# The order of the last root, the last stores and the last scalings at the end of a routed decoder kernel

## Chip, cores and metric

The kernel runs on one core of a Trainium2 chip. The metric is the device time of one execution in microseconds (us), as the median of several executions. Times "in the span" are counted from the first instruction of the profiled execution. PE is TensorE, DVE is VectorE, ACT is ScalarE, POOL is GpSimd, SP is SyncE.

## What is computed

1024 tokens of width 256 go through attention with a residual and a layer norm, a per-token choice of one of four experts by token id with residual and layer norm, and a feed-forward layer in which a router chooses one of four experts. The part that matters here is the last layer norm:

```python
def _layernorm(x, axis=-1, eps=1e-05):
    m = jnp.mean(x, axis=axis, keepdims=True)
    v = jnp.var(x, axis=axis, keepdims=True)
    return (x - m) / jnp.sqrt(v + eps)

x = _layernorm(x + _L0_ffn_ref(x, Wr, br, Wg, Wu, Wd), axis=-1)
```

## The kernel before

The tokens of the last layer lie sorted by expert in T = 10 tiles of 128 rows. Each tile passes four quarters of the feed-forward width; the fourth quarter ends a tile, and only there is the last layer norm done, tile by tile, in the order `last_order` = 0 to 5, 9, 6, 7, 8. The text numbers the tiles by their place n in this order, from 0 to 9, so "row block 7" is the eighth to finish. (The title of the change counts from one: its seventh tile is n = 6, its eighth n = 7, its ninth n = 8.)

For each n the work is spread over three engines, and every engine runs its own list strictly in the order in which it was written out by hand:

- DVE adds PE's product to the sum (`finish_sum`, L1520), takes the row statistics (`finish_stats`, L1526), makes mean and variance of them and adds epsilon (`finish_variance`, L1529 and L1247, which signals `var_ready`, or `last_var` for n = 8 and 9).
- For n = 0 to 7, POOL raises the variance to the power -0.5 (`root`, L500, into `rstd`, signals `rstd_ready`); DVE forms the shift, minus mean times that root (`finish_norm`, L1545, signals `nmr_ready`); ACT scales and shifts the rows (`norm_row`, L1114, signals `out_ready`).
- For n = 8 and 9 (the last `ROOTS_BY_ACT` = 2) ACT takes the square root instead (L1143, into `sroot`, signals `last_root`), for which it has switched its table with a small dummy Sqrt at L1138. DVE takes the reciprocal (L1537) and scales the rows itself (L1538; both `finish_row`, which signals `last_ready`).
- POOL sends every block to its tokens' places in memory with an indirect store (L577), which waits for `out_ready` or `last_ready`.

`mv`, `rstd` and `nmr` have two buffers, used in turn by n. POOL's list in the kernel before takes root n + 1 ahead of store n, for n = 0 to 6; at its end it reads: root 6, store 5, root 7, store 6, store 7, store 8, store 9. ACT's list at its end reads: scaling 6, dummy Sqrt with its table load, scaling 7, root 8, root 9. DVE's list reads: sum 8, statistics 8, shift 7, variance 8, sum 9, statistics 9, scaling 8, variance 9, scaling 9. SP waits for all ten stores (L438), and this ends the kernel.

Of the kernel before, what the change touches and what calls it, by code (L numbers as in the profile page):

```python
# [31 lines left out]
T = MOST - 1  # L32
# [35 lines left out]
def route_kernel(nc, aw, xT_in, x_in, ids_in, wr_in, br_in, ctx_in, ctxn_in, wffn_in, out):  # L68
# [3 lines left out]
    with ExitStack() as ctx:  # L72
# [190 lines left out]
        ROOTS_BY_ACT = 2  # L263


        LN1, LN3 = 0, CHUNKS
# [57 lines left out]
        def pieces_beside(j):  # L324
            q, n = divmod(j, T)
            if q == NQ - 1:
                return range(0)
            a = (q + 1) * Q_PIECES + sum(share[q][:n])
            return range(a, a + share[q][n])
# [112 lines left out]
        def _(pool):  # L442
# [55 lines left out]
            def root(n, buf, i):  # L498
                pool.wait_ge(var_ready, n + 1)
                g.tensor_tensor(out=rstd[:, buf, i:i + 1], in0=mv[:, buf, i, 1:2], in1=mhalf[:, 0:1],  # L500
                                op=ALU.pow).then_inc(rstd_ready, 1)
# [66 lines left out]
                    split(k)  # L568
            root(LN3, 0, 0)
            for n, t in enumerate(last_order):  # L570
                if n + 1 < T - ROOTS_BY_ACT:
                    root(LN3 + n + 1, (n + 1) % 2, 0)
                if n < T - ROOTS_BY_ACT:
                    pool.wait_ge(out_ready, n + 1)
                else:
                    pool.wait_ge(last_ready, n + 1 - (T - ROOTS_BY_ACT))
                g.indirect_dma_start(out=out, out_offset=bass.IndirectOffsetOnAxis(ap=outidx[:, t:t + 1], axis=0),  # L577
                                     in_=buf[:, t, 0:D], in_offset=None, bounds_check=TOKENS - 1,
                                     oob_is_err=False).then_inc(d_out, 16)


        @block.tensor
# [364 lines left out]
        def _(act):  # L947
# [27 lines left out]
            def split(k):  # L975

                n, _, src, hi, _ = all_pieces[k]
                if n == BESIDE:
                    act.wait_ge(d_beside, 16 * PIECES)
                else:  # L980
                    act.wait_ge(d_chunk[slot(n)], 16 * filling(n))
                if n >= E:
                    act.wait_ge(y_done, T + (n // E - 1) * T - 1)
                a(hi, src, ACT.Copy).then_inc(split_hi, 1)  # L984
# [105 lines left out]
            def fxhi(t):  # L1090
                act.wait_ge(x_done, T + t + 1)
                if t == JOINT:
                    a(x_joint[:, 0:P], fX[t % 2][:, 0:P], ACT.Copy).then_inc(xhi_done, 1)
                else:
                    a(x2s(t, 0), fX[t % 2][:, 0:D], ACT.Copy).then_inc(xhi_done, 1)

            def fsilu(j):
                act.wait_ge(g_done, T + j + 1)
                act.wait_ge(h_done, T + j - 1)
                a(gate[:, (T + j) % 2, :], fA[j % 2][:, 0:FQ], ACT.Silu).then_inc(silu_done, 1)  # L1100

            def fhhi(j):
                act.wait_ge(ht_done, T + j + 1)
                act.wait_ge(y_done, T + j - 1)
                if items[j][1] == JOINT:
                    a(h_joint[:, 0:P], fH[j % 2][:, 0:P], ACT.Copy).then_inc(hhi_done, 1)
                else:
                    a(hT[:, j % 2, 0, :], fH[j % 2][:, 0:FQ], ACT.Copy).then_inc(hhi_done, 1)  # L1108

            def norm_row(n):  # L1110

                t = last_order[n]
                act.wait_ge(nmr_ready, n + 1)
                a(buf[:, t, 0:D], buf[:, t, 0:D], ACT.Identity, bias=nmr[:, n % 2:n % 2 + 1],  # L1114
                  scale=rstd[:, n % 2, 0:1]).then_inc(out_ready, 1)

            fxhi(0)
            for i in range(len(items) + 4):
                if i == EARLY:
                    fhhi(i - 1)  # L1120
                    fxhi(i)
                    fxhi(i + 1)
                    fsilu(i)
                else:
                    if i + 1 < JOINT and i + 1 != EARLY:
                        fxhi(i + 1)
                    if i < len(items):
                        fsilu(i)
                    if i + 1 == JOINT:
                        fxhi(i + 1)  # L1130
                    if 1 <= i <= len(items):
                        fhhi(i - 1)
                n = i - 3 - (len(items) - T)
                if 0 <= n < T - 4:
                    norm_row(n)
                if n == T - 3:
                    norm_row(n - 1)
                    a(lsum[:, 0:1], ones_f[:, 0:1], ACT.Sqrt)  # L1138
                if n == T - 2:
                    norm_row(n - 1)  # L1140
                    for k in range(ROOTS_BY_ACT):
                        act.wait_ge(last_var, k + 1)
                        a(sroot[:, k:k + 1], mv[:, (T - ROOTS_BY_ACT + k) % 2, 0, 1:2], ACT.Sqrt).then_inc(last_root, 1)  # L1143
                if i < len(items):
                    for k in pieces_beside(i):
                        split(k)
# [3 lines left out]
        def _(dve):  # L1150
# [3 lines left out]
            def step(ins):  # L1154

                steps[0] += 1
                ins.then_inc(dve_step, 1)
                dve.wait_ge(dve_step, steps[0])
# [87 lines left out]
            def variance_eps(buf, i):  # L1246
                return v.scalar_tensor_tensor(out=mv[:, buf, i, 1:2], in0=mv[:, buf, i, 1:2], scalar=EPS,  # L1247
                                              in1=ones_f[:, 0:1], op0=ALU.add, op1=ALU.mult)
# [150 lines left out]
            def late_blocks(a, b):  # L1399
                block_table(a, b, a - EARLY, nth_by_size[:], 2 * BLOCKS)  # L1400
# [79 lines left out]
            def fhlo(j):  # L1480
                dve.wait_ge(hhi_done, j + 1)
                if items[j][1] == JOINT:
                    v.tensor_copy(h_joint[:, P:FQ], fH[j % 2][:, P:FQ]).then_inc(hlo_done, 1)
                    return
                v.tensor_tensor(out=hT[:, j % 2, 1, :], in0=fH[j % 2][:, 0:FQ],  # L1485
                                in1=hT[:, j % 2, 0, :].bitcast(F32), op=ALU.subtract).then_inc(hlo_done, 1)
# [41 lines left out]
            def finish_variance(n):  # L1528
                step(v.bn_aggr(mv[:, n % 2, 0, :], stats[:, n % 2, :]))  # L1529
                variance_eps(n % 2, 0).then_inc(last_var if n >= T - ROOTS_BY_ACT else var_ready, 1)  # L1530
# [10 lines left out]
            def finish_norm(t):  # L1541
                dve.wait_ge(rstd_ready, LN3 + t + 1)
                if t >= 2:
                    dve.wait_ge(out_ready, t - 1)
                v.scalar_tensor_tensor(out=nmr[:, t % 2:t % 2 + 1], in0=mv[:, t % 2, 0, 0:1], scalar=-1.0,  # L1545
                                       in1=rstd[:, t % 2, 0:1], op0=ALU.mult, op1=ALU.mult).then_inc(nmr_ready, 1)

            for i in range(len(items) + 3):
                if i == EARLY:
                    fhlo(i - 1)  # L1550
                    fxlo(i)
                    fxlo(i + 1)
                    fhidden(i)
                else:
                    if 1 <= i and i + 1 < JOINT and i + 1 != EARLY:
                        fxlo(i + 1)
                    if i == 1:
                        late_blocks(LATE, MOST)
                    if i < len(items):
                        fhidden(i)  # L1560
                    if i + 1 == JOINT:
                        fxlo(i + 1)
                    if 1 <= i < len(items):
                        fhlo(i - 1)
                if i == 1:
                    late_rows(LATE, MOST)
                if 2 <= i <= len(items) + 1 - T:
                    fsum(i - 2)
                if i == T - 1:
                    shifted_logits()  # L1570
                if i == T + 2:
                    gates()
                n = i - 2 - 3 * T
                if 1 <= n <= T - 3:
                    finish_norm(n - 1)
                if 0 <= n < T:
                    finish_sum(n)
                if n == T - 3:
                    fhlo(len(items) - 1)
                if 0 <= n < T:  # L1580
                    finish_stats(n)
                if n == T - 2:
                    finish_norm(n - 1)
                if n == T - 1:
                    dve.wait_ge(out_ready, n - 2)
                    finish_row(n - 1)
                if 0 <= n < T:
                    finish_variance(n)
                if n == T:
                    finish_row(n - 1)  # L1590

# [40 lines left out]
```

## Time and profile before

| what | us |
|---|---|
| median of 3 runs | 183.04 |
| lowest and highest of them | 182.78, 183.89 |
| the profiled execution, its own time | 183.68 |
| its span, first to last instruction | 182.0 |
| so outside the span | 1.68 |

The granted clock of TensorE was 0.988 of full speed on the mean of the span. The timeline gives each instruction's start and duration; the brackets give the idle time of the engine ahead of it and what ended it, where "issue" is time in which it waited for nothing that the profile shows. The chain of waits follows the end of the kernel back: it names at each step what released it.

### The profile page before, as it was taken

The numbers are of one execution on the slowest core, as the hardware profiler recorded it, in microseconds if no ns is written. First come the engines' busy times: TensorE is split into PE (matmuls) and PEld (weight loads), VectorE is DVE, ScalarE is ACT, GpSimd is POOL, SyncE is SP. The second block draws the span as 40 slices with busy tenths as digits, with TensorE's granted clock in tenths as the row PEclk, the third lists the DMA queues.
The fourth block names the chain that finished last, engine by engine and source line by source line (L and its number), as shares of the span: only waits on it lengthen the run. The fifth ranks groups of instructions, "written<-read, shape, count | busy, mean of one in ns | idle before, by whom it ended". The sixth has DMA issues, their size and how long they took to land.

```text
span 182.0 us, 3735 instructions
## 1 busy us (share of the span) xinstructions
PE 169.0 (93%) x947; PEld 125.8 (69%) x947; DVE 123.1 (68%) x393; ACT 95.0 (52%) x246; POOL 104.7 (58%) x125
## 2 busy tenths in 40 slices
PE   7999998899998999999999999999999999999910
PEld 2687776457876643878877788867888587867710
DVE  3388788869686777755655374444699966877780
ACT  3257979625466614347783466635666322545540
POOL 8100666552918574225997999953688700365563
PEclk9999999999999999999999999999999999999995
DMA  4999999257899723156937675274860004411101
GB/s 141 373 312 422 382 389 356 77 150 199 327 342 370 289 100 95 53 132 248 315 95 266 192 326 177 81 260 183 297 217 7 4 0 150 199 58 58 50 27 44
DMA packets 14405, 35.30 MB, mean 194 GB/s; under 512 B 1838, under 2 KB 8112, under 8 KB 14258
## 3 DMA queue, kind: packets, MB, share of 16 engines
q1 hardware_dynamic: 12752, 31.84, 50.3%
q0 software_dynamic: 1344, 3.22, 4.9%
q8 instruction: 10, 0.16, 0.4%
q14 instruction: 9, 0.07, 0.1%
q10 hardware_dynamic: 290, 0.01, 0.1%
HBM read 26.44 MB, written 8.88 MB: 194 GB/s over the span
## 4 chain that ended last, share of the span: by engine, by line
PE 72%; issue 8%; POOL 8%; DVE 5%; DMA 3%; ACT 1%; POOLq 1%; DVEq 0%
PE bank L588 12%; PE bank L589 11%; PE bank L590 11%; PE bank L596 6%; PE bank L786 4%; POOL out_tokens L577 4%; PE bank L901 4%; PE bank L878 3%; POOL rstd L500 3%; PE bank L749 3%; PE bank L659 3%; PE bank L690 3%; PE bank L602 2%; DMA x_sorted<-buf,slot 2%; PE bank L891 2%
## 5 line engine op out<-in xcount | busy, mean ns | idle before, releaser
L496 POOL TENSOR_TENSOR w_lo<-stage,w_hi 128x512 fp32r<-128x512 f32 x40 | 50.9, 1298 | 22.1 <-ACT w_hi L984 17.0
L1100 ACT ACTIVATE gate<-bank 128x256 f32<-128x256 f32 x40 | 15.4, 385 | 42.0 <-PE bank L590 36.4
L1477 DVE TENSOR_TENSOR hid<-bank,gate 128x256 f32<-128x256 f32 x40 | 17.0, 425 | 29.4 <-ACT gate L1100 29.1
L588 PE MATMUL bank<-w_hi,xr 128*128 x72 | 29.6, 411 | 0.5 <-DVE xr L1411 0.3
L500 POOL TENSOR_TENSOR rstd<-mv,mhalf 128x1 f32<-128x1 f32 x16 | 9.7, 604 | 34.1 <-DVE mv L1247 34.1
L589 PE MATMUL bank<-w_lo,xr 128*128 x72 | 28.4, 394 | 0.0
L590 PE MATMUL bank<-w_hi,xr 128*128 x72 | 28.2, 392 | 0.0
L984 ACT ACTIVATE w_hi<-stage 128x512 fp32r<-128x512 f32 x45 | 26.9, 631 | 1.4 <-PE bank L590 0.9
L588 PE MATMUL bank<-w_hi,hT 128*128 x72 | 23.4, 324 | 0.1
L589 PE MATMUL bank<-w_lo,hT 128*128 x72 | 20.3, 282 | 0.0
L590 PE MATMUL bank<-w_hi,hT 128*128 x72 | 20.3, 282 | 0.0
L588 PEld LDWEIGHTS bank<-w_hi,xr 128*128 128x128 f32 x72 | 13.6, 189 | 4.4 <-issue 2.7
L901 PEld LDWEIGHTS bank<-ident,hid 128*128 128x128 f32 x80 | 10.7, 140 | 8.1 <-issue 3.2
L596 PE MATMUL bank<-ones 128*128 128x512 bf16 x54 | 14.8, 426 | 1.1 <-POOL ones L448 1.1
L590 PEld LDWEIGHTS bank<-w_hi,xr 128*128 128x128 f32 x72 | 13.5, 188 | 3.1
L901 PE MATMUL bank<-ident,hid 128*128 128x128 f32 x80 | 15.6, 276 | 0.0
L540 POOL DMA_INDIRECT x_sorted<-buf,slot x10 | 10.1, 1011 | 9.0 <-DVE slot L1363 6.5
L1485 DVE TENSOR_TENSOR hT<-bank,hT 128x256 fp32r<-128x256 f32 x36 | 15.0, 416 | 0.4 <-ACT hT L1108 0.4
L589 PEld LDWEIGHTS bank<-w_lo,xr 128*128 128x128 f32 x72 | 13.6, 189 | 1.5
L1108 ACT ACTIVATE hT<-bank 128x256 fp32r<-128x256 f32 x36 | 13.7, 380 | 0.9 <-PE bank L901 0.9
L588 PEld LDWEIGHTS bank<-w_hi,hT 128*128 128x128 f32 x72 | 13.7, 190 | 0.7 <-issue 0.7
L589 PEld LDWEIGHTS bank<-w_lo,hT 128*128 128x128 f32 x72 | 13.8, 191 | 0.0
(228 smaller groups left out, 342.4 us busy)
## 6 DMA issues: line engine op xcount, KB each, us to landing
stage<-in_w_ffn SPq DMA_DIRECT2D x15, 768.0 KB, 6.0
arena<-in_w_ffn SPq DMA_DIRECT2D x8, 768.0 KB, 5.0
rows<-x_sorted SPq DMA_DIRECT2D x19, 132.0 KB, 2.3
x_sorted<-xr SPq DMA_DIRECT2D x2, 1056.0 KB, 7.1
x_sorted<-xr SPq DMA_DIRECT2D x1, 1584.0 KB, 14.3
buf<-in_x_tok SPq DMA_DIRECT2D x1, 1024.0 KB, 11.6
w_hi<-in_ctx SPq DMA_DIRECT2D x1, 1024.0 KB, 11.8
w_hi<-in_ctxT SPq DMA_DIRECT2D x1, 1024.0 KB, 14.3
```

The lines of the kernel that those rows point to most:

```text
L496: g.tensor_tensor(out=lo, in0=src, in1=hi.bitcast(F32), op=ALU.subtract).then_inc(split_lo, 1)
L500: g.tensor_tensor(out=rstd[:, buf, i:i + 1], in0=mv[:, buf, i, 1:2], in1=mhalf[:, 0:1], op=ALU.pow).then_inc(rstd_ready, 1)
L588: mm(dst, xhi, whi, start=start, stop=False)
L589: mm(dst, xhi, wlo, start=False, stop=False)
L590: return mm(dst, xlo, whi, start=False, stop=stop)
L596: mm(bank[2][:, :].rearrange("p (a b) -> p a b", a=4), ones[:], idle_rhs, start=True, stop=True)
L901: last = tr(fH[j % 2][:, k * P:(k + 1) * P], hid[:, (T + j) % 2, k * P:(k + 1) * P], ident[:])
L984: a(hi, src, ACT.Copy).then_inc(split_hi, 1)
L1100: a(gate[:, (T + j) % 2, :], fA[j % 2][:, 0:FQ], ACT.Silu).then_inc(silu_done, 1)
L1108: a(hT[:, j % 2, 0, :], fH[j % 2][:, 0:FQ], ACT.Copy).then_inc(hhi_done, 1)
L1477: v.tensor_tensor(out=hid[:, (T + j) % 2, :], in0=fA[j % 2][:, FQ:2 * FQ], in1=gate[:, (T + j) % 2, :], op=ALU.mult).then_inc(h_done, 1)
L1485: v.tensor_tensor(out=hT[:, j % 2, 1, :], in0=fH[j % 2][:, 0:FQ], in1=hT[:, j % 2, 0, :].bitcast(F32), op=ALU.subtract).then_inc(hlo_done, 1)
```

## The change

Three orders in the ending are changed; no operation is added, removed or resized.

1. POOL: store 6 is issued ahead of root 7. The list's end becomes root 6, store 5, store 6, root 7, store 7, store 8, store 9. The roots 1 to 6 keep their places.
2. ACT: root 8 comes ahead of scaling 7. The list's end becomes scaling 6, dummy Sqrt, root 8, scaling 7, root 9.
3. DVE: shift 7 comes behind variance 8. The list becomes sum 8, statistics 8, variance 8, shift 7, sum 9 and so on.

```diff
@@ gpsimd: the ending @@
             for n, t in enumerate(last_order):
-                if n + 1 < T - ROOTS_BY_ACT:
+                if n + 2 < T - ROOTS_BY_ACT:
                     root(LN3 + n + 1, (n + 1) % 2, 0)
                 if n < T - ROOTS_BY_ACT:
                     pool.wait_ge(out_ready, n + 1)
...
                                      oob_is_err=False).then_inc(d_out, 16)
+                if n + 2 == T - ROOTS_BY_ACT:
+                    root(LN3 + n + 1, (n + 1) % 2, 0)
@@ scalar: the ending @@
                 if n == T - 2:
-                    norm_row(n - 1)
                     for k in range(ROOTS_BY_ACT):
                         act.wait_ge(last_var, k + 1)
                         a(sroot[:, k:k + 1], mv[:, (T - ROOTS_BY_ACT + k) % 2, 0, 1:2], ACT.Sqrt).then_inc(last_root, 1)
+                        if k == 0:
+                            norm_row(n - 1)
@@ vector: the ending @@
                 if 0 <= n < T:
                     finish_stats(n)
-                if n == T - 2:
-                    finish_norm(n - 1)
                 if n == T - 1:
                     dve.wait_ge(out_ready, n - 2)
                     finish_row(n - 1)
                 if 0 <= n < T:
                     finish_variance(n)
+                if n == T - 2:
+                    finish_norm(n - 1)
```

## Rows read from the trace of the kernel before

**Rows 1.** The page: span, and busy time of each engine (us, share of the span, instructions).
```profile
span 182.0 us, 3735 instructions
...
PE 169.0 (93%) x947; PEld 125.8 (69%) x947; DVE 123.1 (68%) x393; ACT 95.0 (52%) x246; POOL 104.7 (58%) x125
```

**Rows 2.** The chain that ended last, its final pieces: start us, us, what.
```profile
174.08 0.90 POOL out_tokens L577
174.98 0.73 issue
...
177.80 1.55 POOLq L72
```

**Rows 3.** Timeline of POOL, last 12 us: start us, us, operation, [idle before <-releaser].
```profile
170.90 1.04 POOL L577 DMA_INDIRECT out_tokens<-buf,outidx  x1 [0.20 <-issue]
173.32 0.57 POOL L500 TENSOR_TENSOR rstd<-mv,mhalf 128x1 f32<-128x1 f32 x1 [1.38 <-DVE mv L1247]
174.08 1.04 POOL L577 DMA_INDIRECT out_tokens<-buf,outidx  x1 [0.19 <-issue]
175.71 0.97 POOL L577 DMA_INDIRECT out_tokens<-buf,outidx  x1 [0.59 <-issue]
176.98 1.09 POOL L577 DMA_INDIRECT out_tokens<-buf,outidx  x1 [0.30 <-issue]
178.38 0.97 POOL L577 DMA_INDIRECT out_tokens<-buf,outidx  x1 [0.30 <-issue]
```

**Rows 4.** Timeline of ACT, the same stretch.
```profile
171.92 0.59 ACT L1114 ACTIVATE buf<-buf,nmr,rstd 128x256 f32<-128x256 f32 x1
172.53 1.28 ACT L1138 ACT_TABLE_LOAD   x1
173.82 0.20 ACT L1138 ACTIVATE lsum<-ones_f 128x1 f32<-128x1 f32 x1
174.31 0.60 ACT L1114 ACTIVATE buf<-buf,nmr,rstd 128x256 f32<-128x256 f32 x1 [0.29 <-DVE nmr L1545]
174.82 0.19 ACT L1143 ACTIVATE sroot<-mv 128x1 f32<-128x1 f32 x1
```

**Rows 5.** Timeline of DVE, the same stretch.
```profile
173.07 0.16 DVE L1247 SCALAR_TENSOR_TENSOR mv<-mv,ones_f 128x1 f32<-128x1 f32 x1
...
173.66 0.43 DVE L1526 BATCH_NORM_STATS2 stats<-buf 128x6 f32<-128x256 f32 x1
174.12 0.16 DVE L1545 SCALAR_TENSOR_TENSOR nmr<-mv,rstd 128x1 f32<-128x1 f32 x1
...
174.41 0.16 DVE L1247 SCALAR_TENSOR_TENSOR mv<-mv,ones_f 128x1 f32<-128x1 f32 x1
174.48 0.48 DVE L1520 SCALAR_TENSOR_TENSOR buf<-bank,topw,arena 128x256 f32<-128x256 f32 x1
...
175.66 0.41 DVE L1538 TENSOR_SCALAR buf<-buf,mv,rstd 128x256 f32<-128x256 f32 x1
...
176.82 0.41 DVE L1538 TENSOR_SCALAR buf<-buf,mv,rstd 128x256 f32<-128x256 f32 x1
```

**Rows 6.** Timeline of POOL, earlier indirect stores (attention's and second layer's ends).
```profile
35.21 0.72 POOL L500 TENSOR_TENSOR rstd<-mv,mhalf 128x1 f32<-128x1 f32 x1 [0.69 <-DVE mv L1247]
36.32 1.05 POOL L505 DMA_INDIRECT x_sorted<-buf,slot  x1 [0.39 <-issue]
...
54.92 1.13 POOL L540 DMA_INDIRECT x_sorted<-buf,slot  x1 [3.60 <-DVE slot L1363]
56.07 0.76 POOL L534 TENSOR_TENSOR buf<-ve,mhalf 128x2 f32<-128x2 f32 x1
```

**Rows 7.** Timeline of DVE, the writers that those stores waited for.
```profile
35.05 0.48 DVE L1264 SCALAR_TENSOR_TENSOR buf<-buf,mv,rstd 128x256 f32<-128x256 f32 x1
35.97 0.48 DVE L1264 SCALAR_TENSOR_TENSOR buf<-buf,mv,rstd 128x256 f32<-128x256 f32 x1 [0.44 <-POOL rstd L500]
...
53.84 0.17 DVE L1363 TENSOR_REDUCE slot<-pos 128x3 int32<-128x15 f32 x1
```

## Prediction, made before the changed kernel ran

> **What bounds the kernel now.** I read the page first. Over the span PE is the busiest engine, 169.0 of 182.0 us [rows 1], but all three edits lie behind the last matmuls, so the shares of the span say nothing about them. The view that decides is the chain that ended last, read from its end backwards: its last pieces are the stores on POOL and the wait for the last one to land [rows 2]. Then I laid the timelines of POOL, ACT and DVE over the same 12 us [rows 3 to 5], and asked of each POOL instruction: was it started by its own data, or by POOL coming free?
>
> - Root 7 started at 173.32, just behind its variance, whose second instruction ran from 173.07 to 173.23 [rows 3, 5]. Data set it. POOL had been idle since store 5 ended at 170.90 + 1.04 = 171.94.
> - Store 6 ran from 174.08 to 175.12 behind root 7 [rows 3]. Its rows had been ready since scaling 6 ended, 171.92 + 0.59 = 172.51 [rows 4]. So it lay 1.6 us behind its data; this is the slack that the change goes for.
> - Store 7 started at 175.71. POOL was free from 175.12, and scaling 7 had ended at 174.31 + 0.60 = 174.91 [rows 3, 4]. The chain puts the release at 174.98 and then 0.73 us of "issue" [rows 2].
> - Stores 8 and 9 started 0.30 us behind the end of the store ahead of each (176.98 and 178.38), though their rows were scaled by 176.07 and 177.23 [rows 3, 5]. They are set by POOL alone, so the end is store 7's start plus a fixed 178.38 - 175.71 = 2.67 us, plus store 9's own 0.97 and its landing: 182.0 - 178.38 = 3.62 us.
>
> So the question is one number: when does store 7 start? What holds for it is the path root 7, shift 7, scaling 7, store 7.
>
> **A price that must be read first: from ready rows to a store's start.** Behind a root, a store starts 0.19 us after the root's end (173.89 to 174.08, or root 35.93 to 36.32 with 0.39) [rows 3, 6]. That looks cheap, but there its rows may have been ready long before. Where the store's own data came last, the gap is longer: 174.91 to 175.71 is 0.80 us [rows 3, 4]; DVE's scaling 35.05 + 0.48 = 35.53 to the store at 36.32 is 0.79; DVE's slot numbers 53.84 + 0.17 = 54.01 to the store at 54.92, with POOL idle, is 0.91 [rows 6, 7]. So a store costs 0.79 to 0.91 us between its last data and its start when nothing covers this. Call it w; I take 0.80, from the row in the same ending. In the old order of store 6 root 7 covered it: the two starts are 0.76 us apart, 0.57 of which is the root [rows 3]. In the new order nothing covers it, because store 6 waits for nothing but its own rows.
>
> The Trainium skill (DMA: Bandwidth & Descriptors, section "Anatomy of one DMA — SWDGE (gpsimd) path") gives about 50 ns for the sequencer's dispatch, and says that the fixed cost is dominated by completion, not by setup; by this w would be near 0.05 and the change a gain. No row here shows so small a w. The Trainium skill's page Perfetto Trace Analysis, section "DMA Instruction — SWDGE (GPSIMD)", adds that such an instruction has no start marker, only an end; then w and the store's duration can only be trusted as a sum.
>
> The sum of the two, by ends alone, is 176.68 - 174.91 = 1.77 for store 7 and 56.05 - 54.01 = 2.04 for the store at 54.92 [rows 3, 4, 6, 7].
>
> **The change part by part.** Nothing is added or removed; the durations stay.
>
> *Store 6 ahead of root 7 (POOL).* Root 6, store 5 and scaling 6 are untouched, so the rows are ready at 172.51 as before, with POOL idle since 171.94. Store 6 starts at 172.51 + 0.80 = 173.31 and takes 1.04: it ends at 174.35 (174.28 to 174.55 by the bounds 1.77 and 2.04). Only this one instruction is moved; root 7 is what it is moved past. A root can follow a store's end at 0.02 us (56.05 to 56.07) [rows 6]; its variance, done at 173.23, is long there. Root 7 runs from 174.37 to 174.94, which is 1.05 us later than the 173.32 of before.
>
> *Shift 7 (DVE).* Before, the root ended at 173.89 and shift 7 started at 174.12, held for its last part by statistics 8 (173.66 + 0.43 = 174.09) [rows 3, 5]. Now DVE waits for the root. The gap from a root's end to a DVE instruction that waits for it is 0.04 us (35.93 to 35.97) [rows 6, 7], at most the 0.23 of before. Shift 7 runs from 174.98 to 175.14, 0.86 later than before. The 0.19 that the root's delay loses here is slack that DVE's queue had.
>
> *What stands behind shift 7 on DVE.* Sum 9, which started at 174.48 [rows 5]. By the edit variance 8 is now ahead of the shift, directly behind statistics 8, and finishes at about 174.49, 0.08 earlier than before (174.41 + 0.16 = 174.57). Behind the shift sum 9 starts at about 174.98 + 0.08 = 175.06, 0.58 later than before, and everything after it on DVE moves by the same 0.58: scaling 8 ends at 176.07 + 0.58 = 176.65, scaling 9 at 177.23 + 0.58 = 177.81.
>
> *Root 8 ahead of scaling 7 (ACT).* Root 8 was at 174.82, behind scaling 7 [rows 4]. Now it starts behind its variance at about 174.52 and is over by 174.71, while ACT waits for shift 7 anyway. It costs nothing, and by itself it buys nothing: DVE uses root 8 only behind statistics 9, about 176.0 on the new clock. If this order had not been changed, root 8 would run behind scaling 7, 175.77 to 175.96, still before DVE asks for it. So the parts on ACT and DVE are worth 0 (bounds: 0.08 gained on variance 8, off the path; on the loss side 0.19, root 8's own duration, if it collided with scaling 7).
>
> *Scaling 7 and store 7.* ACT starts 0.03 us after the shift's end (174.28 to 174.31) [rows 4, 5]: 175.17, ending at 175.77. Now w is due a second time: store 7 starts at 175.77 + 0.80 = 176.57. Store 6 is long gone (174.35), so nothing else holds it.
>
> *Sum.* 176.57 - 175.71 = +0.86 us for store 7. Stores 8 and 9: store 7 ends at 176.57 + 0.97 = 177.54, plus 0.30 gives store 8 at 177.84 (its rows were ready at 176.65, and 176.65 + 0.80 = 177.45 is earlier); store 9 at 177.84 + 1.39 = 179.23 (its rows: 177.81 + 0.80 = 178.61, earlier). Both keep POOL's distances. So the end moves by +0.86 us: span 182.86, this execution 184.54 by its own time. The profiled execution lies 0.64 above the median of 183.04, so for the median I say 183.04 + 0.86 = 183.9 us, 0.5% slower.
>
> By the bounds: root 7 starts between 174.30 and 174.57, the DVE step adds up to 0.19, and the second w between -0.01 and 0.11. The shift of the end is then 0.78 to 1.36 us, 183.8 to 184.4.
>
> Put generally: store 7 starts at 172.51 + w + 1.04 + 0.02 + 0.57 + 0.04 + 0.16 + 0.03 + 0.60 + w = 174.97 + 2w, against 175.71. The change pays only if w is under 0.37. What it wins is that store 6 no longer lies between root 7 and store 7; what it loses is that root 7, the head of the path, waits for store 6 and no longer for its variance alone, and that both waits for rows lie open.
>
> **Rivals.**
>
> *Faster: w is short (7 in 100).* If the 0.20 behind a root (0.19 read) is the true price of a store's start, store 7 starts at 174.97 + 0.40 = 175.37, the end moves by -0.34 us: 182.7. For it: POOL has been idle and its sequencer may have prepared store 6. Against it: store 7 itself, 0.59 us behind store 6's end when the usual gap is 0.30, with its data coming last. It decides below w = 0.37. By the 50 ns of the Trainium skill (the page on DMA, above) it would be 175.07, -0.64 us, 182.4.
>
> *No difference (11 in 100).* Store 6 has a head start, since POOL can prepare it in the idle time from 171.94, so only the second w is due in full: 174.97 + 0.20 + 0.80 = 175.97, +0.26 us: 183.3. For it: root 7 covers most of the price in the old order. Against it: the store at 54.92 also found POOL idle and paid 0.91.
>
> *Slower by more: ACT switches its table (3 in 100).* If scaling 7 between two roots needed another table, 1.28 us [rows 4] would fall in front of it: load 174.71 to 175.99, scaling to 176.59, store 7 at 177.39, +1.68 us: 184.7. Against it: the dummy root at 173.82, scaling at 174.31 and root at 174.82 ran in this mix with no load between [rows 4].
>
> *Slower by more: DVE becomes the bound (4 in 100).* Sum 9 now waits for POOL's root. Store 9's rows have 179.23 - 178.61 = 0.62 us to spare; a stall of the shift beyond that, 1.2 us in all, would give 184.5 and more. Nothing in DVE's list shows such a stall.
>
> **How the numbers follow.** My forecast (+0.78 to +1.36 us) has 75 in 100, and its likeliest value is 183.9. The other cases have 11, 7, 4 and 3. The median of three runs moves too: those shown lie between 182.78 and 183.89. The range 183.0 to 184.6 takes in the forecast, the case of no difference and some of that spread, and leaves out the gain and the table load. About 1% (1.8 us) is what a measurement here can tell from no change. Neither the gain (at most 0.64) nor the forecast reaches it. Faster by over 1%: 0.01; within 1%: 0.93; slower by over 1%: 0.06, from the table load and a long stall of DVE, with some spread on top.
>
> **What would show it.** Store 6 near 173.3, about a microsecond ahead of root 7's start near 174.4; scaling 7 near 175.2 on ACT; store 7 near 176.6, with POOL idle for over 1.5 us ahead of it; then stores at 0.30 gaps. Variance 8 ahead of shift 7, sum 9 near 175.1, root 8 near 174.5, no second table load. The forecast is wrong if store 6 starts within 0.4 us of 172.51, or if store 7 starts at or before 175.71.

## The result, and the profile of the changed kernel

The changed kernel took 183.73 us (median of 16 executions) against 182.80 us for the kernel before (16 executions, the runs shown above among them). The ratio of the two is 1.0038, with a 95% interval of 1.0019 to 1.0056. On 182.80 us this is 0.69 us slower, between 0.35 and 1.02 us; the two medians lie 0.93 us apart, inside the same interval. One of the 16 executions of the changed kernel was slow (427.12 us) and is left out of the ratio. The forecast was +0.86 us.

The profiled execution of the changed kernel has a span of 181.5 us, shorter than the 182.0 us of before. That is not a gain. Its variance 7 (second instruction, L1250 in its numbering) started at 171.82, where before it started at 173.07 [rows 5]: this execution came to the ending 1.25 us earlier, with nothing changed up to there. So I compare stretches, not clocks. From variance 7's start to the end of the span it was 182.0 - 173.07 = 8.93 us before, and it is 181.5 - 171.82 = 9.68 us now: +0.75 us. The span is given to 0.1 us, so such a difference can be off by up to 0.1 us. Store 9's start, which has two decimals, gives much the same: 178.38 - 173.07 = 5.31 us before and 177.91 - 171.82 = 6.09 us now, +0.78 us.

The timeline of POOL in the changed kernel, last 12 us (start us, us, operation, idle before and what ended it), against [rows 3]:

```profile
169.66 1.04 POOL L577 DMA_INDIRECT out_tokens<-buf,outidx  x1 [0.19 <-issue]
172.06 0.97 POOL L577 DMA_INDIRECT out_tokens<-buf,outidx  x1 [1.37 <-ACT buf L1116]
173.04 0.62 POOL L500 TENSOR_TENSOR rstd<-mv,mhalf 128x1 f32<-128x1 f32 x1
175.29 1.04 POOL L577 DMA_INDIRECT out_tokens<-buf,outidx  x1 [1.63 <-ACT buf L1116]
176.63 0.97 POOL L577 DMA_INDIRECT out_tokens<-buf,outidx  x1 [0.30 <-DVE buf L1541]
177.91 0.97 POOL L577 DMA_INDIRECT out_tokens<-buf,outidx  x1 [0.30 <-issue]
```

ACT in the same stretch, against [rows 4]:

```profile
170.67 0.59 ACT L1116 ACTIVATE buf<-buf,nmr,rstd 128x256 f32<-128x256 f32 x1
171.28 1.28 ACT L1140 ACT_TABLE_LOAD   x1
172.58 0.20 ACT L1140 ACTIVATE lsum<-ones_f 128x1 f32<-128x1 f32 x1
173.28 0.20 ACT L1144 ACTIVATE sroot<-mv 128x1 f32<-128x1 f32 x1 [0.50 <-DVE mv L1250]
173.89 0.60 ACT L1116 ACTIVATE buf<-buf,nmr,rstd 128x256 f32<-128x256 f32 x1 [0.41 <-DVE nmr L1548]
```

DVE, against [rows 5]:

```profile
171.82 0.16 DVE L1250 SCALAR_TENSOR_TENSOR mv<-mv,ones_f 128x1 f32<-128x1 f32 x1
...
173.69 0.16 DVE L1548 SCALAR_TENSOR_TENSOR nmr<-mv,rstd 128x1 f32<-128x1 f32 x1 [0.45 <-POOL rstd L500]
173.77 0.48 DVE L1523 SCALAR_TENSOR_TENSOR buf<-bank,topw,arena 128x256 f32<-128x256 f32 x1
```

And the chain that ended last, against [rows 2]:

```profile
171.33 0.73 issue
172.06 0.97 POOL out_tokens L577
173.03 0.01 issue
173.04 0.63 POOL rstd L500
```

How to read them. Scaling 6 ends at 170.67 + 0.59 = 171.26, POOL has been idle since 170.70, and still store 6 starts only at 172.06: 0.80 us, which the chain shows as 0.73 us of "issue". Root 7 follows store 6's end at once (the bracket is missing: no idle time), 1.06 us behind the end of variance 7 (171.98), where before it followed at 0.09. DVE now idles for the root ("0.45 <-POOL rstd L500"); shift 7 starts at 173.69. Scaling 7 ends at 174.49, and store 7 starts at 175.29, again 0.80 us. POOL has idled 1.63 us ahead of it.

### The profile page after: what moved, and what is told of

It reads as the page before. It is cut to its first block, busy times and chain, and to the rows that moved or that the text cites. A ratio compares the mean times of both kernels' runs of the same rounds, so it can differ in the third digit from the quotient of the medians.

```text
span 181.5 us, 3735 instructions
## 1 busy us (share of the span) xinstructions
PE 167.6 (92%) x947; PEld 125.0 (69%) x947; DVE 123.2 (68%) x393; ACT 94.6 (52%) x246; POOL 104.6 (58%) x125
## 4 chain that ended last, share of the span: by engine, by line
PE 72%; DVE 9%; DMA 5%; issue 4%; POOL 4%; POOLq 1%; ACT 1%; SPq 0%; DVEq 0%
PE bank L590 15%; PE bank L591 14%; PE bank L592 14%; PE bank L903 5%; PE bank L880 4%; DMA x_sorted<-buf,slot 3%; PE bank L788 3%; PE bank L598 3%; DMA rows<-x_sorted 2%; PE bank L751 2%; PE bank L893 2%; PE bank L604 2%; PE bank L661 2%; DVE buf L1257 1%; DVE stats L1260 1%
## 5 line engine op out<-in xcount | busy, mean ns | idle before, releaser
L500 POOL TENSOR_TENSOR rstd<-mv,mhalf 128x1 f32<-128x1 f32 x16 | 9.7, 606 | 31.7 <-DVE mv L1250 31.4
L540 POOL DMA_INDIRECT x_sorted<-buf,slot x10 | 10.1, 1009 | 9.1 <-DVE slot L1366 6.5
```

The costliest lines, as they stand in the source:

```text
L540: g.indirect_dma_start(out=scr2, out_offset=bass.IndirectOffsetOnAxis(ap=slot2[:, t:t + 1], axis=0), in_=buf[:, t, :], in_offset=None, bou ...
```

## The measure used for the experiments

A difference of 0.3 us is less than the spread of the times, but in a trace it is plain. So for each kernel I give two stretches of its profiled execution: from variance 7's start to store 7's start, which holds everything that the orders touch, and from variance 7's start to the end of the span. The ratio of the times stands beside them, to the kernel before on the same chip (12 executions of each kernel e1 to e10, but one of e3; there is no e8). The second stretch ends with the span and carries its rounding.

| kernel | variance 7 to store 7, us | variance 7 to end, us | ratio of times (95%) |
|---|---|---|---|
| before | 175.71 - 173.07 = 2.64 | 8.93 | 1 |
| the change | 175.29 - 171.82 = 3.47 | 9.68 | 1.0038 (1.0019 to 1.0056) |
| e1: POOL's edit alone | 175.85 - 172.35 = 3.50 | 9.75 | 1.0052 (1.0022 to 1.0082) |
| e2: ACT's and DVE's edits alone | 175.03 - 172.09 = 2.94 | 9.11 | 1.0024 (0.9997 to 1.0051) |
| e5: as e1, store 6 not waiting for scaling 6 | 174.97 - 172.31 = 2.66 | 8.89 | 0.9992 (0.9966 to 1.0018) |
| e3: the change, POOL busy ahead of store 7 | 175.91 - 172.43 = 3.48 | 9.67 | one execution |
| e4: before, bound of the last stores in a register | 174.75 - 172.39 = 2.36 | 8.51 | 0.9976 (0.9950 to 1.0001) |
| e6: the change, bound in a register | 174.52 - 172.08 = 2.44 | 8.62 | 0.9989 (0.9958 to 1.0019) |
| e7: before, all stores' bounds in registers | 174.18 - 171.82 = 2.36 | 8.48 | 0.9960 (0.9931 to 0.9988) |
| e10: the same as e7, on another chip | 174.53 - 172.17 = 2.36 | 8.53 | 0.9981 (0.9958 to 1.0004) |
| e9: e7 with POOL's new order and an earlier scaling 6 | 173.69 - 171.55 = 2.14 | 8.35 | 0.9973 (0.9950 to 0.9996) |

## Experiments

**Which edit carries the loss (e1, e2).** e1 is the first two hunks of the change, on POOL, and nothing else; e2 is the other hunks.

> Only the edit on POOL: store 6 ahead of root 7; ACT and DVE as before. Measure: from the start of variance 7's second instruction on DVE to the end of the span, 8.93 us before and 9.68 us with the whole change. Theory (the loss is all POOL's; the edits on ACT and DVE are worth nothing beside it): store 6 about 0.8 us behind the end of scaling 6, root 7 behind store 6, ending 9.6 to 9.8 us, time 0.75 to 0.9 us over before. Rival (the edits on ACT and DVE carry part of the loss): ending at 9.4 us or less. Other rival (they hold off a further loss, since variance 8 now waits behind shift 7): 9.9 us or more.

> Only the edits on ACT and DVE; POOL as before, root 7 ahead of store 6. Theory: shift 7 now waits for statistics 8 and both steps of variance 8, about 0.29 us later than before, and scaling 7 waits behind root 8 on ACT; scaling 7 starts 0.31 to 0.43 us later, store 7 0.80 us behind its end, so the ending grows from 8.93 to 9.24 to 9.36 us. Rival (these two edits are free in every order): ending 8.9 to 9.0 us.

e1's POOL timeline:

```profile
172.59 0.97 POOL L577 DMA_INDIRECT out_tokens<-buf,outidx  x1 [1.37 <-ACT buf L1116]
173.57 0.59 POOL L500 TENSOR_TENSOR rstd<-mv,mhalf 128x1 f32<-128x1 f32 x1
175.85 1.04 POOL L577 DMA_INDIRECT out_tokens<-buf,outidx  x1 [1.69 <-ACT buf L1116]
```

e1 is the change again: 3.50 us against 3.47, 9.75 against 9.68. The loss is POOL's edit, whole. The 0.03 us between them are no more than such rows differ by from one trace to the next.

In e2 root 7 has its old place, and in its trace the other two edits cost by themselves. From e2's DVE and ACT (its L1248 and L1546 are variance 8 and shift 7; L1142 and L1114 are root 8 and scaling 7):

```profile
173.35 0.16 DVE L1248 SCALAR_TENSOR_TENSOR mv<-mv,ones_f 128x1 f32<-128x1 f32 x1
173.43 0.16 DVE L1546 SCALAR_TENSOR_TENSOR nmr<-mv,rstd 128x1 f32<-128x1 f32 x1
```

```profile
173.54 0.20 ACT L1142 ACTIVATE sroot<-mv 128x1 f32<-128x1 f32 x1 [0.50 <-DVE mv L1248]
173.65 0.59 ACT L1114 ACTIVATE buf<-buf,nmr,rstd 128x256 f32<-128x256 f32 x1
```

Shift 7 starts 1.34 us behind variance 7, where before it was 174.12 - 173.07 = 1.05 [rows 5]; it now stands behind variance 8. Scaling 7 stands behind root 8. Store 7 comes 0.30 us later (2.94 against 2.64), just under the expected 0.31 to 0.43. The whole ending grew by 0.18 only, under my 9.24 to 9.36: store 8 took 0.97 us in e2 and 1.09 us in the kernel before [rows 3], which the last section comes back to. In times e2 can't be told from before. So "worth nothing" holds only behind the late root of the new order; in the old order these two edits delay store 7 by 0.30 us in the trace.

**Is it the order, or the late rows of store 6 (e5)?** e5 has POOL's edit; store 6 does not wait for scaling 6, whose result goes to a spare tile (block 6 leaves the kernel unscaled; the durations stay).

```diff
-                    pool.wait_ge(out_ready, n + 1)
+                    pool.wait_ge(out_ready, n if n == T - 4 else n + 1)
...
-                a(buf[:, t, 0:D], buf[:, t, 0:D], ACT.Identity, bias=nmr[:, n % 2:n % 2 + 1],
+                a(spare[:] if n == T - 4 else buf[:, t, 0:D], buf[:, t, 0:D], ACT.Identity, bias=nmr[:, n % 2:n % 2 + 1],
```

> POOL's edit alone, and in it store 6 does not wait for scaling 6: ACT writes the scaled rows of block 6 to a spare tile, and store 6 sends the rows unscaled (so block 6's output is not normalised). Theory (what the new order costs is only that root 7 waits for a store whose rows come late): store 6 starts 0.3 us behind store 5 and ends before variance 7, root 7 starts within 0.1 us of its variance as before, store 7 starts where it did, ending 8.85 to 9.0 us. Rival (the order itself costs, since POOL now idles ahead of store 7 and must be woken for it): store 7 later than 0.80 us behind scaling 7, ending 9.2 us or more.

```profile
171.49 0.98 POOL L578 DMA_INDIRECT out_tokens<-buf,outidx  x1 [0.30 <-issue]
172.56 0.57 POOL L501 TENSOR_TENSOR rstd<-mv,mhalf 128x1 f32<-128x1 f32 x1
174.97 1.04 POOL L578 DMA_INDIRECT out_tokens<-buf,outidx  x1 [1.84 <-ACT buf L1117]
```

Store 6 ends at 172.47, as variance 7 does, root 7 follows at 0.09 us, and the loss is gone: 2.66 us against 2.64. The order itself costs nothing. Nor does an idle POOL: it had idled 1.84 us ahead of store 7, which still came 0.81 us behind scaling 7 (which ended at 173.56 + 0.60 = 174.16). Taking store 6 out from between root 7 and store 7 did not help either, because store 7 was never held by it: its 0.80 us ran beside it.

**What the 0.80 us are (e3, e4).** In e3 a power of one column, whose result nobody reads, stands between the wait for scaling 7 and store 7:

```diff
+                if n == 7:
+                    g.tensor_tensor(out=spare[:, 0:1], in0=ones_f[:, 0:1], in1=mhalf[:, 0:1], op=ALU.pow)
                 g.indirect_dma_start(out=out, out_offset=bass.IndirectOffsetOnAxis(ap=outidx[:, t:t + 1], axis=0),
```

> The whole change, and a power of one column (0.57 us on POOL, its result unused) between the wait for scaling 7 and store 7. Theory (the 0.80 us behind the wait are not POOL's own work, so POOL can do something else in them): store 7 starts 0.76 to 0.85 us behind the end of scaling 7, as without it, the ending 9.6 to 9.8 us. Rival (POOL itself is at work in them, or waking up): store 7 starts 1.3 to 1.4 us behind scaling 7, ending 10.2 us or more.

```profile
175.18 0.54 POOL L579 TENSOR_TENSOR spare<-ones_f,mhalf 128x1 f32<-128x1 f32 x1 [0.91 <-ACT buf L1119]
175.91 1.04 POOL L580 DMA_INDIRECT out_tokens<-buf,outidx  x1 [0.20 <-issue]
```

Scaling 7 ended at 175.10. The extra power started 0.08 us behind it and took 0.54 us, and store 7 started 0.81 us behind scaling 7, as without it. So at least 0.5 of the 0.80 us are not work of POOL's compute side, and not a wake-up: they belong to something ahead of it in the queue. (The last 0.20 us, behind the power, are the gap that stores show behind a root [rows 3].) This is also how root 7 hides store 6's price in the old order.

The candidate was in the trace all along. In the following view of the kernel before, from 174 to 179 us (duration ns, first and last start us), POOLq is POOL's sequencer. It runs a 29 ns MOVE for each of the stores 7, 8 and 9, at the moment when that store's rows are ready (174.9, 176.1, 177.3). Store 6's MOVE lies ahead of the view, at 173.27.

```profile
L577 POOL DMA_INDIRECT out_tokens<-buf,outidx x4: 971/1004/1091, 174.1 to 178.4; - x4
L577 POOLq MOVE  x3: 29/29/29, 174.9 to 177.3; - x3
```

I read it as the instruction that writes the constant of `bounds_check` to a register, and that carries the wait; in e4, where the constant has a register of its own, the same line of the program shows no MOVE. e4 is the kernel before with that register written once, ahead of all ten stores:

```diff
             root(LN3, 0, 0)
+            last_token = pool.to_reg(TOKENS - 1)
...
-                                     in_=buf[:, t, 0:D], in_offset=None, bounds_check=TOKENS - 1,
+                                     in_=buf[:, t, 0:D], in_offset=None, bounds_check=last_token,
```

> The kernel before, with the bound of the last ten indirect stores put in a register once, so that no MOVE stands between a store's wait and the store. Rival (the 0.8 us between ready rows and the store's start is the sequencer's work behind the wait, the MOVE above all, and could be done ahead): store 7 starts 0.30 us behind the end of store 6, as the others do, the ending falls from 8.93 to about 8.64 us. Theory (the 0.8 us belong to the store instruction itself and start when its wait ends): the gap from scaling 7's end to store 7's start stays 0.75 to 0.80 us, ending 8.85 to 8.95 us.

```profile
173.41 1.04 POOL L578 DMA_INDIRECT out_tokens<-buf,outidx  x1 [0.20 <-issue]
174.75 0.97 POOL L578 DMA_INDIRECT out_tokens<-buf,outidx  x1 [0.30 <-issue]
```

Store 7 starts 0.30 us behind store 6's end, 0.51 us behind scaling 7 (173.64 + 0.60 = 174.24), now held by store 6 and not by its rows. My theory in this expectation fell: the price is not the store's own. The rival was right on store 7 (-0.28 us), and the ending fell by 0.42 us, more than its 0.29. Of the rest, 0.12 us is store 8, 0.97 us here against 1.09 [rows 3]. Store 7 gained no more than 0.28 us because store 6 became what it waits for.

**The store's price laid open (e6).** The change with the same register.

> The whole change, with the bound of the last ten stores in a register (no MOVE between wait and store). This lays the store's price open where nothing covers it: call w' the gap from scaling 6's end to store 6's start, with POOL idle. From variance 7 to store 7's start it is 2.64 us before, 3.47 with the change, 2.36 in e4. By my sum it should now be 1.90 + 2w'. Rival of the prediction (a store's own price is small once its wait is the last thing ahead of it): w' 0.05 to 0.25 us, so 2.0 to 2.4 us, and the new order is at least as fast as the old one with the same register. Theory (the register only helps behind a running store; a store on an idle POOL still pays): w' 0.4 to 0.8 us, 2.7 to 3.5 us, slower than e4.

```profile
171.80 0.97 POOL L578 DMA_INDIRECT out_tokens<-buf,outidx  x1 [0.85 <-ACT buf L1117]
172.78 0.58 POOL L500 TENSOR_TENSOR rstd<-mv,mhalf 128x1 f32<-128x1 f32 x1
174.52 1.04 POOL L578 DMA_INDIRECT out_tokens<-buf,outidx  x1 [1.15 <-ACT buf L1117]
```

```profile
170.93 0.59 ACT L1117 ACTIVATE buf<-buf,nmr,rstd 128x256 f32<-128x256 f32 x1
173.65 0.58 ACT L1117 ACTIVATE buf<-buf,nmr,rstd 128x256 f32<-128x256 f32 x1
```

Scaling 6 ended at 170.93 + 0.59 = 171.52 and scaling 7 at 173.65 + 0.58 = 174.23. The stores follow at 0.28 and 0.29 us. So of the 0.80 us, 0.28 are due in any case, and 0.52 go away with the MOVE. The ends of the stores, which do not rest on the start that the trace shows, say the same. From the end of the scaling to the end of its store it is 1.77 us (store 6) and 1.84 us (store 7) in the changed kernel, and 1.25 us (172.77 - 171.52) and 1.33 us (175.56 - 174.23) in e6. My two cases for w' left out just this value (0.05 to 0.25, or 0.4 to 0.8); the prediction's sum for store 7, counted from variance 7's start, is 174.97 - 173.07 + 2w = 1.90 + 2w, and it holds: 1.90 + 2 x 0.28 = 2.46 us against 2.44 measured. The change costs 0.83 us with the MOVE and 0.08 us without it (2.44 against e4's 2.36). With the register the two orders can't be told apart in times (0.9989 and 0.9976, with intervals that overlap).

**Registers for all stores (e7, e10).**

> The old order, with the bounds of all 28 indirect stores in registers. In the ending the same as e4: 2.36 us from variance 7 to store 7. Theory (the price behind the wait is paid only where a store's rows come last): stores whose rows come last at the ends of the first two layers start 0.2 to 0.6 us earlier; some of this reaches the time through the loads of the sorted rows, 0 to 0.8 us beyond e4, so 0.3% to 0.6% under before in all. Rival (the layers between hide it): e4's time within 0.1%.

> The old order with the bounds of all stores in registers, once more, as the neighbour of e9 on the same chip: 2.36 us from variance 7 to store 7, the time 0.3% to 0.6% under before.

Both show 2.36 us. The times are 0.40% and 0.19% under before, in the first case clear of noise, in the second at its edge and less than the 0.3% to 0.6% that I expected. That the same kernel gives both says how far such times can be trusted. How much the earlier layers add to e4's gain stays open. There the register did less than I had thought. In the first layer three of the four stores behind a root started earlier but ended no earlier (the very first did end 0.28 us earlier behind its root). One of the three, from e7, to be set beside the store at 36.32 [rows 6], which was 1.05 us long and 0.39 us behind its root:

```profile
35.38 1.25 POOL L505 DMA_INDIRECT x_sorted<-buf,slot  x1 [0.18 <-issue]
```

The store ends 1.43 us behind the root's end here (36.63 - 35.20) and 1.44 before (37.37 - 35.93): the start moved up by 0.2 us and the row grew by as much. The first store of the second layer's end and the slot numbers that it waited for, in e7:

```profile
53.79 1.12 POOL L541 DMA_INDIRECT x_sorted<-buf,slot  x1 [3.52 <-DVE slot L1365]
```

```profile
52.79 0.17 DVE L1365 TENSOR_REDUCE slot<-pos 128x3 int32<-128x15 f32 x1
```

52.96 to 53.79 is still 0.83 us, where before it was 0.91 [rows 6, 7]. These stores wait for two things, slots and rows (L538 and L539 in the kernel before), and the slots come last. The sequencer's row ahead of this store, from the view of e7's L540, the line of the second wait, from 52 to 54 us (duration ns, first and last start us):

```profile
L540 POOLq EVENT_SEMAPHORE  x1: 822/822/822, 52.2 to 52.2; - x1
```

This is an instruction of the sequencer that waits, from 52.2 to 53.0 us, until the slots are there. The store starts about 0.8 us behind its end, with no MOVE between. So the price stands here with another instruction of the sequencer that holds the last wait, and does not seem bound to writing a constant. This is read from the rows of one kernel; no experiment takes the second wait away.

**The new order, with its conditions met (e9).** e5 says what POOL's order needs: store 6 over before variance 7 is there. In e9, with the registers of e7 and POOL's new order, shift 6 moves one place up on DVE, ahead of `fhlo(38)` (the low half of a tile's hidden rows), and scaling 6 one place up on ACT, ahead of `fhhi(39)` (the copy of the last tile's hidden rows). The diff leaves out the edits that it shares with e7 and with the change:

```diff
+                    if i == len(items):
+                        norm_row(T - 4)
                     if 1 <= i <= len(items):
                         fhhi(i - 1)
...
                 if n == T - 3:
-                    norm_row(n - 1)
                     a(lsum[:, 0:1], ones_f[:, 0:1], ACT.Sqrt)
...
+                    if i == len(items) - 1:
+                        finish_norm(T - 4)
                     if 1 <= i < len(items):
                         fhlo(i - 1)
...
-                if 1 <= n <= T - 3:
+                if 1 <= n <= T - 4:
                     finish_norm(n - 1)
```

> Registers for the bounds of all stores, store 6 ahead of root 7 on POOL (ACT and DVE keep the old order of root 8, scaling 7, shift 7 and variance 8), and shift 6 and scaling 6 each one place earlier, so that block 6's rows are ready while store 5 still runs. Theory (the new order costs nothing once store 6 is over before variance 7 is there, and then takes store 6 out of the way between root 7 and store 7): scaling 6 ends about 0.7 us earlier, store 6 starts 0.3 us behind store 5, root 7 starts within 0.15 us of variance 7, and from variance 7 to store 7's start it takes 2.1 to 2.25 us, against 2.36 in the old order with registers; 0.1 to 0.2 us less in all, which the times can hardly tell from the old order with registers. Rival (the earlier shift and scaling hold up the last products and DVE): variance 7 comes later behind statistics, or stores 8 and 9 wait for their rows; 2.3 us or more, or gaps over 0.30 us ahead of stores 8 or 9.

```profile
169.34 1.04 POOL L579 DMA_INDIRECT out_tokens<-buf,outidx  x1 [0.20 <-issue]
170.68 0.98 POOL L579 DMA_INDIRECT out_tokens<-buf,outidx  x1 [0.30 <-issue]
171.80 0.57 POOL L500 TENSOR_TENSOR rstd<-mv,mhalf 128x1 f32<-128x1 f32 x1
173.69 1.04 POOL L579 DMA_INDIRECT out_tokens<-buf,outidx  x1 [1.32 <-ACT buf L1118]
```

Scaling 6 ends at 170.24, store 6 runs from 170.68 to 171.66, right behind store 5, and root 7 starts 0.09 us behind variance 7 (171.55 + 0.16). From variance 7 to store 7 it is 2.14 us, 0.22 us under e7 and e10, and the ending is 8.35 us, 0.58 us under before. Of the 0.22 us, 0.16 are left at store 9's start (176.30 - 171.55 = 4.75 us against 176.73 - 171.82 = 4.91 in e7), since store 7 took 1.04 us here and 0.97 there. e9's time is 0.9973 (0.9950 to 0.9996) of before: it is below both kernels of this case, though against the kernel before only just clear of noise. Beside e10 on the same chip (0.9981) it can't be told apart in times; its lead over the old order with registers rests on the trace alone. So POOL's new order does bring something, once a store costs 0.28 us and store 6's rows are early.

## Why the prediction was right, point by point

- *What bounds the ending.* Right. Every kernel above that moved store 7 moved the end with it: 6.1 to 6.3 us lie between store 7's start and the end of the span in all of them (6.29 before, 6.21 with the change).
- *w = 0.80 us, due at both bare waits.* Right as a size: 0.80 us twice in the changed kernel. I called it the price of a store, and that was wrong in kind: 0.52 us of it go away with the MOVE that holds the wait (e4, e6), and 0.28 us stay. The size came from a row with the same MOVE in the same ending, so that the number was right does not show that the cause was understood. The forecast did not need the cause, but an engineer would, since the 0.52 can be taken away. The price of 0.91 us, taken from the second layer as an upper bound, belonged to a store with two waits, and so to another case.
- *Store 6 and root 7.* Expected at 173.31 and 174.37 on the clock of before; on that clock (1.25 us added) they came at 173.31 and 174.29. Store 6 took 0.97 us and not 1.04: in the ending the rows show 1.04 only where POOL's instruction before the store was a root, however long ago, as for store 7 here. Root 7 took 0.62 and not 0.57, so the two errors nearly cancel, which is luck. The sum by ends, 1.77 us from scaling 6 to the end of store 6, was met as it stood (173.03 - 171.26).
- *Shift 7 and scaling 7.* Expected at 174.98 and 175.17; they came at 174.94 and 175.14. The gap from root to waiting DVE was 0.03 us (0.04 expected).
- *Store 7.* Expected at 176.57, came at 176.54: +0.83 us against +0.86.
- *Stores 8 and 9.* Right that POOL alone sets them, 0.30 us behind each other. But from store 7's start to store 9's it took 177.91 - 175.29 = 2.62 us in place of the fixed 2.67: store 8 took 0.97 us and not 1.09, and store 7 took 1.04 and not 0.97. So 0.78 us of the 0.83 reached store 9's start; 0.75 us by the span, with its rounding. This distance was called fixed, and it lies between 2.54 and 2.67 us in the kernels above.
- *The bounds, +0.78 to +1.36 us.* The traces reached only their lower end (0.75 to 0.83 us), and the ratio of the times, 0.69 us, lies below it with an interval of 0.35 to 1.02. The larger part of the distance to the upper end came from the store with two waits (0.20 and 0.11 of 0.50 us). The time itself, 183.73 us, is well inside the stated 183.0 to 184.6. That a measurement here tells only about 1% from no change was too cautious: 16 executions of each kernel told 0.38%.
- *Root 8 ahead of scaling 7, shift 7 behind variance 8, worth 0.* Right inside the change (e1: 0.03 us), though in e2's trace they cost 0.30 us where root 7 is on time.
- *The rivals.* "w is short" was the right question: e6 put w at 0.28 us. By the prediction's limit ("the change pays only if w is under 0.37") it should have paid there, and it still cost 0.08 us (2.44 against 2.36). The limit was wrong, because it left the old order at 175.71, a time that itself holds a w of 0.80. With a short w the old order gains too, until store 6's end plus 0.30 us holds store 7: 2.36 us in e4. By 1.90 + 2w = 2.36 I estimate the true limit at w = 0.23 us. The rule from the Trainium skill (page DMA: Bandwidth & Descriptors, "Anatomy of one DMA — SWDGE (gpsimd) path", about 50 ns for the dispatch) did not decide it: 0.28 us was the least that a run showed from ready rows to a store's start. "Store 6 has a head start" fell: it paid 0.80 us in full with POOL idle. No second table load came; its +1.68 us would have been 0.9%, so alone it did not belong to "slower by over 1%". Nor did DVE become the bound.

## What to carry to other kernels

Before a transfer is moved ahead of a short operation on its queue, look up when its data are ready: the saving counts from there, and if the operation that is passed heads the path that sets the end, it now waits for that data too. Read the gap behind the last wait at a place where nothing covers it; the 0.19 us behind a root said nothing of the 0.80 us that were due in the open. And look at what stands between a wait and the instruction that it guards: a constant that is written to a register there, again for every transfer, cost 0.5 us where it lay bare and the store could have started, and writing it once ahead of the loop took 0.42 us off the ending (8.93 to 8.51), over half of the 0.75 us that the reordering had put on. Judge such a gain by the ends of the stores too: in the first layer three of four starts moved up by 0.2 us behind their roots and the ends did not.

## What the runs showed of the hardware that was not expected

- With a 29 ns MOVE of the sequencer between a wait and an indirect store, the store starts 0.80 us behind its last data; without it the same store starts 0.28 to 0.29 us behind (e6, two places, POOL idle at both). In e7 a store whose last data were awaited by another sequencer instruction (EVENT_SEMAPHORE, 0.82 us) started 0.83 us behind them with no MOVE there. The 0.52 us can run beside another operation of POOL (e3, one execution: a power of 0.54 us in them, and store 7 no later).
- In three of the first layer's four stores behind a root, leaving the MOVE out brought the start forward from 0.39 to 0.18 or 0.19 us behind the root, while the row grew from 1.05 to 1.25 or 1.26 us, so that the end stayed (e7 against [rows 6]).
- In the ending an indirect store's row is 0.97 to 0.98 us long behind another store and 1.04 us behind a root, but for store 8. Store 8 took 1.09 us before and 1.02 us in e1 and e5. In these three store 9's rows came ready while store 8 ran (before: 177.23, with store 8 from 176.98 to 178.07), so that the MOVE fell into it. It took 0.97 us in e2, e3 and the change, where the MOVE came ahead of it (the change: rows ready at 176.51, store 8 from 176.63), and in all kernels with registers, which have no MOVE there. A MOVE beside a running store is not enough to lengthen it, though: in the kernel before, store 8's MOVE came at 176.1, beside store 7 (175.71 to 176.68), which took 0.97 us. What lengthens store 8 stays open.
